# Causal attention: future keys set to zero behind the exponential instead of masked in front of it

## The reference, cut to what matters

```python
scores = jnp.einsum('bnqh,bnkh->bnqk', q, k) / scale
causal = jnp.tril(jnp.ones((l, l), bool))
scores = jnp.where(causal, scores, jnp.finfo(scores.dtype).min)
attn = jax.nn.softmax(scores, axis=-1)
ctx = jnp.einsum('bnqk,bnkh->bnqh', attn, v)
```

## Time and profile before

| what | us |
|---|---|
| median of 3 runs (lowest to highest) | 2140.19 (2139.48 to 2140.79) |
| the profiled execution | 2137.56 |
| its span, first to last instruction | 2135.8 |
| from the first step of `rot` to its last, in the trace | about 480 to 697 |
| TensorE busy / VectorE / ScalarE / GpSimd, of the span | 68% / 69% / 39% / 27% |

### The profile page before, as it was taken

One profiled execution on the slowest core, in us unless ns is written; L12 is line 12 of the kernel. 1 busy time (PEld: TensorE's weight loads), 2 busy tenths in 40 slices (PEclk: granted clock), 3 DMA queues, 4 the chain that ended last, 5 costly groups with the idle time before them and its releaser, 6 DMA issues. The chain is left out here.

```text
span 2135.8 us, 35245 instructions
## 1 busy us (share of the span) xinstructions
PE 1445.6 (68%) x10364; PEld 861.4 (40%) x10397; DVE 1470.7 (69%) x4775; ACT 825.2 (39%) x2043; POOL 583.4 (27%) x1036
## 2 busy tenths in 40 slices
PE   6488887958888614999809266766676666667651
PEld 3122224524444412666505144544454445445540
DVE  3578885657777620111135499989998999899955
ACT  2266664215555301222203244444444544454430
POOL 4100001210000032000063245444554455445530
PEclk9699998969999856999958657666766677666765
DMA  5572220352330511111134600110021002100001
GB/s 161 170 258 78 75 71 8 113 153 70 79 78 21 244 45 55 45 44 44 44 102 142 172 7 1 48 33 2 1 50 31 2 1 55 26 2 1 2 1 40
DMA packets 87485, 137.61 MB, mean 64 GB/s; under 512 B 9720, under 2 KB 68000, under 8 KB 85540
## 3 DMA queue, kind: packets, MB, share of 16 engines
q1 hardware_dynamic: 84068, 127.38, 20.2%
q0 software_dynamic: 3264, 8.41, 1.2%
HBM read 82.50 MB, written 53.76 MB: 64 GB/s over the span
## 5 line engine op out<-in xcount | busy, mean ns | idle before, releaser
L1420 DVE MATCH_REPLACE8 top_left<-top_next,top_left 128x65 f32<-128x65 f32 (+15 forms) x768 | 321.9, 427 | 0.0
L1415 DVE MAX8 top_next<-top_left 128x8 f32<-128x65 f32 (+15 forms) x768 | 300.5, 431 | 0.0
L1346 POOL TENSOR_TENSOR top_e<-top_e,top_left 128x129 f32<-128x129 f32 (+15 forms) x256 | 191.2, 769 | 209.0 <-DVE top_left L1420 209.0
L1212 ACT ACTIVATE top_e<-top_ps_s,top_neg_max 128x129 f32<-128x129 f32 (+15 forms) x256 | 125.3, 489 | 284.7 <-POOL top_neg_max L1331 271.0
L686 DVE TENSOR_REDUCE tok_rowmax<-tok_ps_s 128x1 f32<-128x512 f32 x256 | 166.9, 688 | 42.8 <-PE tok_ps_s L528 40.2
L1097 PE MATMUL top_ps_pt<-ident,top_e 128*128 128x128 f32 x640 | 145.6, 354 | 70.0 <-issue 40.9
L1973 DVE TENSOR_TENSOR moe_hid<-moe_act_gate,moe_ps_h 128x512 f32<-128x512 f32 x39 | 26.8, 687 | 220.3 <-ACT moe_act_gate L1934 220.3
L686 DVE TENSOR_REDUCE rot_rowmax<-rot_ps_s 128x1 f32<-128x128 f32 (+3 forms) x256 | 115.6, 487 | 46.5 <-PE rot_ps_s L531 42.5
L659 ACT ACTIVATE tok_et<-tok_ps_st 128x1024 f32<-128x1024 f32 x128 | 124.2, 1021 | 51.0 <-PE tok_ps_st L562 51.0
L1873 PE MATMUL moe_ps_h<-moe_w,moe_rows_t 128*128 x312 | 142.7, 601 | 0.4 <-issue 0.4
L1097 PEld LDWEIGHTS top_ps_pt<-ident,top_e 128*128 128x128 f32 x640 | 101.4, 182 | 92.6 <-issue 87.6
(11 more groups left out here) (343 smaller groups left out, 3151.6 us busy)
## 6 DMA issues: line engine op xcount, KB each, us to landing
moe_w<-in_moe_w SPq DMA_DIRECT2D x3, 4096.0 KB, 24.3
moe_xs<-zeros SPq DMA_DIRECT2D x1, 5120.0 KB, 20.8
last_xs<-zeros SPq DMA_DIRECT2D x1, 5120.0 KB, 33.8
moe_rows<-moe_xs SPq DMA_DIRECT2D x40, 128.0 KB
moe_ys<-moe_y SPq DMA_DIRECT2D x38, 128.0 KB, 1.7
v_rows<-tok_va SPq DMA_DIRECT2D x4, 1024.0 KB, 5.1
tok_vs<-v_rows SPq DMA_DIRECT2D x16, 256.0 KB
v_rows<-rot_va SPq DMA_DIRECT2D x4, 1024.0 KB, 5.0
```

Of the source, the lines that this page charges most:

```text
L1212: act.activation(e[:, U % KEPT, 0:keys(U)], row(U), ACT.Exp, bias=neg_max[:, U % 4:U % 4 + 1]).then_inc(e_ok, 1)
L1346: pool.tensor_tensor(e[:, U % KEPT, 0:w], e[:, U % KEPT, 0:w], left[:, U % 4, 0:w], ALU.subtract).then_inc(prob_ok, 1)
L1415: dve.max(next8[:, U % 2, step // 2, :], left[:, U % 4, 0:keys(U)]).then_inc(pick, 1)
L1420: ins = dve.match_replace(left[:, U % 4, 0:w], next8[:, U % 2, step // 2 - 1, :], left[:, U % 4, 0:w], 0.0)
```

## The change

The second pass gets no mask product: `second` issues line 562's product alone, and `mask_kq` and its two instructions in `constants` are gone. Behind the exponentials of a key block, GpSimd executes one `affine_select` over the 128 x 128 diagonal block of all four heads in `et` (128 partitions, 4 x 128 elements, in place), which keeps an element where the query is not earlier than the key and writes 0.0 elsewhere. There are 64 of them, one for each step and key block. Each waits for both exponentials of its block, and counts up a new semaphore `past_ok`. `values` of the causal attention waits for `past_ok` in place of `exp_ok`. The maxima of the first pass are masked as before, so an exponential of a later key may be any number until it is overwritten.

```diff
+        past_ok = c.sem(st, f"{tag}_past_ok")
...
+            if causal:
+                for n in range(B * G * NQ):
+                    kt = n % NQ
+                    at = slice(kt * P, kt * P + P)
+                    pool.wait_ge(exp_ok, 2 * n + 4)
+                    pool.affine_select(out=et[:, kt % 2, :, at], in_=et[:, kt % 2, :, at], compare_op=ALU.is_ge, fill=0.0,
+                                       base=0, pattern=[[0, HG], [1, P]], channel_multiplier=-1).then_inc(past_ok, 1)
...
                     mm = pe.matmul(ps_st[:, h, q_from(kt):], k[:, h, k0 + kt * P:k0 + kt * P + P],
-                                   q[:, h, q_from(kt):], start=True, stop=not causal)
-                    if causal:
-                        mm = pe.matmul(ps_st[:, h, kt * P:kt * P + P], c.ident_bf[:, :], c.mask_kq[:, :],
-                                       start=False, stop=True)
+                                   q[:, h, q_from(kt):], start=True, stop=True)
                 mm.then_inc(st_mm, 1)
...
-                pe.wait_ge(exp_ok, b * (G * 8) + (g * 8 + 2 * kt + 4))
+                if causal:
+                    pe.wait_ge(past_ok, b * (G * NQ) + (g * NQ + kt + 1))
+                else:
+                    pe.wait_ge(exp_ok, b * (G * 8) + (g * 8 + 2 * kt + 4))
```

More of the change, by code:

```diff
@@ L120, in constants @@
     c.mask_qk = c.sbuf(c.stack, "mask_qk", [P, P], BF16)
-    c.mask_kq = c.sbuf(c.stack, "mask_kq", [P, P], BF16)
     c.pick_cls = c.sbuf(c.stack, "pick_cls", [B, B, P], F32)
@@ L139, in _ @@
                 pool.memset(c.mask_qk[:, :], 0.0).then_inc(filled, 1)
-                pool.memset(c.mask_kq[:, :], 0.0).then_inc(filled, 1)
                 pool.memset(c.pick_cls[:, :, :], 0.0).then_inc(filled, 1)
-                pool.wait_ge(filled, 5)
+                pool.wait_ge(filled, 4)
                 for ident in (c.ident, c.ident_bf):
@@ L147, in _ @@
                                    base=0, pattern=[[-1, P]], channel_multiplier=1).then_inc(filled, 1)
-                pool.affine_select(out=c.mask_kq[:, :], in_=c.mask_kq[:, :], compare_op=ALU.is_ge, fill=MASKED,
-                                   base=0, pattern=[[1, P]], channel_multiplier=-1).then_inc(filled, 1)
                 pool.affine_select(out=c.pick_cls[:, :, :], in_=c.pick_cls[:, :, :], compare_op=ALU.not_equal,
@@ L152, in _ @@
                                    channel_multiplier=1).then_inc(filled, 1)
-                pool.wait_ge(filled, 10)
+                pool.wait_ge(filled, 8)
                 pool.memset(zeros[:, :, :], 0.0).then_inc(filled, 1)
@@ L163, in _ @@
                           allow_small_or_imprecise_dtypes=True).then_inc(filled, 1)
-                pool.wait_ge(filled, 17)
+                pool.wait_ge(filled, 15)
                 pool.affine_select(out=c.before[:, :], in_=c.before[:, :], compare_op=ALU.is_gt, fill=0.0,
@@ L168, in _ @@
                                    fill=0.0, base=B - 1, pattern=[[0, 1]], channel_multiplier=-1).then_inc(filled, 1)
-                pool.wait_ge(filled, 19)
+                pool.wait_ge(filled, 17)
 def load_step(sp, c, b, g, q, k, loaded):
```

## The result

The changed kernel takes 2143.37 us (median of 9 runs, 2141.22 to 2145.79), the kernel before 2138.78 (9 runs on the same chip, 2134.49 to 2140.79). The ratio, taken from the means of these runs, is 1.0025 with a 95% interval of 1.0015 to 1.0035: slower by 5.3 us (the medians differ by 4.6). The forecast was 4.9 us, and 2145.1 us for the kernel, counted from the 2140.19 us that three runs of before had given; over nine runs that kernel's median is 1.4 us lower.

What follows compares the result with a forecast made beforehand. Causal steps were taken as bound by a loop between engines, neither TensorE nor VectorE full. 4.2 us for 15 boundaries plus 1.1 for the last step less 0.4 for constants gave +4.9, 2145.1 us; range 2139.5 to 2152.5.

Steps and rivals of the forecast that it cites:

- The gain: Causal steps: of 16 removed mask products, only four in front of units 4 and 11 count, 0.22 us a step.
- The price of a select: GpSimd, each of 64 added selects: 0.63 us, taken from one with 4 partitions and 512 elements.
- The hand-overs: Around each select: ScalarE to GpSimd 0.09 us, GpSimd to TensorE 0.05 us.
- Its cost at the tail: Block 3's select delays `values(3)` by 0.61 us and the next step by 0.50 us; blocks 0 to 2 are hidden.
- The net step: Each step boundary: 0.50 us cost less 0.22 us gain, 0.28 us; 15 of them 4.2 us.
- VectorE's stop lies beside and not on top: Step's tail: line 698 stands still beside the select, negated maxima 0.5 us later, the same half microsecond as TensorE's delay.
- The second rival: Step's tail: line 698 goes first, the select waits; 0.75 us a step instead of 0.50, 2148.9 us; chance 0.17.
- The last step: No first pass to hide behind: block 0's select meeting line 747 costs 0.5 us, `values(3)` 0.6, together 1.1 us.
- The first step: Start of the causal attention: counted like the other step boundaries, 0.28 us longer.
- The constants: GpSimd's queue before the stage's barrier: one memset and one select fewer, 0.4 us less.
- The clock: Rival, causal steps: clock falls more often, six more steps at 1.09 us, 6.5 us on top, 2151.6 us; chance 0.13.
- TensorE as the bound: Rival, causal steps: each removed product counts, 0.88 us gained a step against 0.50 cost, 2135.2 us; chance 0.07.

Runs made afterwards that it cites:

- e2: Changed kernel, but block 3 keeps its mask product and `values(3)` waits for the exponentials alone; usual step 13.32 us, ratio 0.9992 to the kernel before.
- e6: Changed kernel, but only blocks 0 and 1 go by the select, blocks 2 and 3 keep their mask products; usual step 13.34 us, ratio 0.9997 to before.
- e3: Changed kernel, but block 3 alone goes by the select, blocks 0 to 2 keep their mask products; usual step 14.04 us, ratio 1.0052 to before.
- e4: Changed kernel, with line 704 reading the class token's scores from PSUM, so one SBUF input; usual step 13.79 us, ratio 1.0024 to before.
- e7: Changed kernel, with the negated maxima turned before `values(3)` and copied before `pv_rows` in causal steps; usual step 13.71 us, one run 2142.54 us.
- e8: Changed kernel with the order of e7 and the PSUM input of e4 together; usual step 13.50 us, ratio 0.9994 to before.
- e1: Kernel before with its mask products kept, the 64 selects and the wait of `values` for them added; usual step 14.18 us, ratio 1.0079 to before.
- e5: Changed kernel with the select of block 3 executed twice, one behind the other; usual step 14.53 us, one run 2178.46 us.
- e10: The kernel of e5, unchanged, in a further execution; 11 of 15 steps long, 2181.53 us in all.

## Why the prediction was right

Point by point, by its own steps:

- **The gain**, 0.22 us a step from the four products in front of units 4 and 11: 0.25 and 0.23 measured (e2, e6). Block 2's products, put at nothing, were worth 0.02 (e6).
- **The price of a select**, 0.63 us: 0.64 or 0.65 in 61 of the 64, 0.73 in the three that began behind VectorE's line 735. **The hand-overs**: ScalarE to GpSimd 0.06 us where 0.09 was taken, GpSimd to TensorE 0.05 as taken.
- **Its cost at the tail**, 0.50 us a step: 0.47 (e3), and nothing for the other blocks (e2). The net step, 0.28 expected, was 0.22.
- **VectorE's stop lies beside and not on top**: e4 shows it (no change), e7 and e8 show that it was as long as the other two chains. By the Trainium skill (SBUF — State Buffer, section "Who interferes with whom") whoever issues first holds the pair of SBUF ports that VectorE and GpSimd share for the whole instruction; line 704, issued 0.10 us behind the select, bears it out with 0.57 us.
- **The second rival had its mechanism right and its size wrong.** A select behind a VectorE instruction with two SBUF inputs is held (0.91 us in e1), but behind line 711, 0.17 us long, it loses 0.02 us and not 0.25. e1's step of 14.18 is explained almost without it: 0.47 us (e3), 0.11 for exponentials that are not earlier, and these 0.02 make 0.60 of its 0.61.
- **The last step** was over-sized: 1.1 us expected on top of the 15 boundaries. Line 753 (747 of before), in the last step, did take 0.88 us instead of 0.42, as it met the select of block 0. But from `pv_rows` to `pv_rows` the step grew by 0.60 only, 9.66 to 10.26. With block 3 alone by select (e3) it is 10.26 too, and with blocks 0 to 2 (e2) 9.89. What failed is the addition: blocks 0 to 2 cost 0.23 us, net, by themselves and nothing more beside block 3's select.
- **The first step** was taken for one like the others, 0.28 us. From the stage's first copy to the first `pv_rows` it became 0.06 us shorter, 13.26 against 13.32. Block 3 by select costs about the same there (e3, 13.88), but the other twelve products bring 0.60 (e2, 12.72), nearly the 0.66 that twelve are worth in a full queue: behind the first exponential of before, TensorE was busy all of 2.33 us, at a clock of 0.50.
- **The constants** gave 0.37 us of the 0.4: the first load was issued at 6.17 us and is at 5.80.
- **The clock** did not fall more often in the changed kernel (one long step in each of two executions and in e4), though each long step cost 1.5 us where 1.09 was taken. The rival's condition is real at longer steps: e5 and e10 show it at 14.53 us, and e1 and e3 fit it.
- **TensorE as the bound**: refuted by e2 for the steps that repeat; for the first step it comes near.

In the trace the first step gives -0.1 us, the 14 behind it 3.1, the last one 0.6 and the constants -0.4: together 3.3 us, where the forecast's own terms had 4.9. The runs say 5.3, with an interval from 3.2 to 7.5. So the mechanism of the usual step was right, and that the total came within 0.4 us of the runs is in part luck. What is missing between 3.3 and 5.3, if anything is, was not found. The interval takes in 3.3, but e4, whose usual step is the same, is by its own runs 5.1 us slower than before, too. Single executions of one kernel differ by 5 us.

## What to carry to other kernels

Work moved off a busy engine gains only where another engine was waiting behind it, here for 4 of 16 products, while a hand-over added at a point where three chains end together costs most of its length (0.61 us a step in e1), and a second one all of it (0.74 in e5). So give the cheap engine the pieces that have something to do behind them, blocks 0 to 2, and leave the last one where it was. When the end of a loop is set by chains of equal length, shorten them together: one alone shows little (0.00 us in e4, 0.08 in e7, 0.29 together in e8). Two engines that read SBUF can hold each other up in either order, so look at which of them starts first.

## What the runs showed of the hardware

- A VectorE instruction with a single SBUF input can stop beside GpSimd too: `tensor_scalar` on 128x16 f32 to bf16 took 0.52 us in e1 and 0.39 in e4 instead of 0.20. The Trainium skill (same page and section) counts `tensor_scalar` among the operations that can run in a mode with two ports. The maxima of the first pass did not stop: four of them, the last of which overlapped the select at 576.81, took 2.39 us together, against 2.40 in the earlier trace rows.
- GpSimd is held too. A select that began 0.01 us behind a VectorE instruction with two SBUF inputs took 0.91 us where that instruction takes 0.42, and 0.66 where it takes 0.17 (e1), instead of 0.63: it ends 0.50 us behind VectorE. One that began 0.02 us behind a VectorE instruction of 0.17 us with one input from PSUM took 0.63 (e1, at 528.28).
- The price of `affine_select` from a row of 4 partitions with 512 elements, 0.63 us, held for 128 partitions: 0.64 us.
- TensorE's clock fell in 10 and 11 of 15 steps once each step had 0.7 us more of waiting in its tail (e5, e10). In e5 the long steps cost more than the second select itself: 235.86 - 204.62 = 31 us in the stage, of which 15 x 0.74 = 11 are the select.
